# Moving low parts and a norm to GpSimd, issuing q's copies first and merging the shift transfers in a cross-attention and mixture-of-experts kernel

## The reference

```python
x = x + xattn(layernorm(x), ctx)      # then x = x + expert_ffn(layernorm(x))
# xattn:
q = ln_head((x @ Wq + bq)) ; k = ln_head(y_main @ Wk + bk) ; v = y_main @ Wv + bv   # 240 keys
k_dca, v_dca = ln_head(...), ...                                                      # 16 more keys
ctx     = softmax(q @ k.T * SCALE) @ v
ctx_dca = softmax(q @ k_dca.T * SCALE) @ v_dca
return (ctx + ctx_dca) @ Wo + bo
```

## Time and profile before

| what | value |
|---|---|
| median of three runs (lowest to highest) | 1104.68 us (1100.12 to 1105.48) |
| the profiled execution | 1106.82 us |
| its span, first to last instruction | 1105.0 us |
| granted TensorE clock, mean | 0.929 |
| TensorE busy | 948.3 us, 86% |
| VectorE busy | 797.6 us, 72% |
| ScalarE busy | 640.0 us, 58% |
| GpSimd busy | 285.1 us, 26% |

### The profile page before, as it was taken

One profiled execution on the slowest core, in us unless ns is written; L12 is line 12 of the kernel. 1 busy time (PEld: TensorE's weight loads), 2 busy tenths in 40 slices (PEclk: granted clock), 3 DMA queues, 4 the chain that ended last, 5 costly groups with the idle time before them and its releaser, 6 DMA issues. The chain is left out here.

```text
span 1105.0 us, 17666 instructions
## 1 busy us (share of the span) xinstructions
PE 948.3 (86%) x5148; PEld 674.2 (61%) x5148; DVE 797.6 (72%) x1723; ACT 640.0 (58%) x1659; POOL 285.1 (26%) x203
## 2 busy tenths in 40 slices
PE   0667899989989988989989989676379999999998
PEld 0334555556556555555555556333369999999997
DVE  3726777778777877777777777551878787878785
ACT  0222887787887887787787788672533232323231
POOL 0465135235235225135135135000000000000000
PEclk9977899999999999999999899777589999999999
DMA  7006435436435535445435435558211111111111
GB/s 266 28 20 144 103 91 158 118 92 159 120 95 153 130 92 146 112 99 158 114 99 157 105 88 131 138 180 261 84 39 58 57 57 57 57 57 57 57 38 39
DMA packets 56413, 116.41 MB, mean 105 GB/s; under 512 B 13944, under 2 KB 22392, under 8 KB 56120
## 3 DMA queue, kind: packets, MB, share of 16 engines
q1 hardware_dynamic: 53760, 115.16, 37.6%
q10 hardware_dynamic: 2616, 0.79, 0.3%
HBM read 47.24 MB, written 17.30 MB: 58 GB/s over the span
## 5 line engine op out<-in xcount | busy, mean ns | idle before, releaser
L477 POOL TENSOR_TENSOR vs<-vs,neg_half 128x16 f32<-128x16 f32 x66 | 191.0, 2916 | 391.9 <-DVE vs L934 391.9
L806 ACT ACTIVATE sc<-sc,nm 128x240 f32<-128x240 f32 x512 | 223.2, 444 | 46.2 <-DVE ed L982 45.4
L977 DVE TENSOR_REDUCE pm<-sc 128x64 f32<-128x1024 f32 x128 | 156.6, 1223 | 69.5 <-PE sc L633 65.2
L584 PE MATMUL ring<-wq,xT 128*128 128x512 f32 x256 | 142.5, 708 | 22.8 <-ACT xT L774 18.4
L633 PE MATMUL sc<-KS,QS 96*128 96x256 f32 x512 | 109.5, 339 | 54.8 <-ACT sc L806 44.1
L815 ACT ACTIVATE pt<-sc 128x1024 f32<-128x1024 f32 x128 | 124.2, 1024 | 33.7 <-PE sc L654 33.7
L1421 ACT ACTIVATE hb<-hb 128x352 f32<-128x352 f32 x64 | 31.9, 498 | 186.9 <-DVE hb L1477 186.9
L633 PEld LDWEIGHTS sc<-KS,QS 96*128 96x128 f32 x512 | 75.8, 201 | 98.8 <-ACT sc L806 60.1
L686 PE MATMUL ring<-wo,ot 128*128 128x512 f32 x256 | 124.7, 612 | 0.7 <-DVE ot L1030 0.7
L806 ACT ACTIVATION_READ_ACCUMULATOR sc<-sc,nm 128x1 f32 x512 | 110.8, 216 | 0.0
L584 PEld LDWEIGHTS ring<-wq,xT 128*128 128x128 f32 x256 | 55.8, 230 | 88.3 <-issue 63.8
(11 more groups left out here) (144 smaller groups left out, 1796.8 us busy)
## 6 DMA issues: line engine op xcount, KB each, us to landing
KS<-k_hi SPq DMA_DIRECT2D x128, 128.0 KB, 2.3
QS<-q_hi SPq DMA_DIRECT2D x128, 128.0 KB, 3.9
xin<-in_x_dram SPq DMA_DIRECT2D x16, 512.0 KB, 4.0
KS<-k_lo SPq DMA_DIRECT2D x64, 128.0 KB, 2.3
QS<-q_lo SPq DMA_DIRECT2D x64, 128.0 KB, 3.5
xres<-in_x_dram SPq DMA_DIRECT2D x16, 512.0 KB, 4.1
x_scratch<-xres SPq DMA_DIRECT2D x16, 512.0 KB, 4.3
x<-x_scratch SPq DMA_DIRECT2D x16, 512.0 KB, 3.2
```

What stands on the lines that cost most here:

```text
L477: pool.tensor_tensor(w, w, neg_half[0:rows, :], ALU.pow).then_inc(rstd, 1)
L584: last = pe.matmul(bank[:, :], xT[:, kc, t * P:(t + 1) * P], wq[:, kc, :], start=(kc == 0), stop=(kc == KC - 1))
L806: last = act.activation(s, s, ACT.Exp, bias=nm[:, t, h:h + 1], accum_out=den[:, t, h:h + 1])
L977: dve.tensor_reduce(pieces, s.rearrange("p h (c n) -> p h c n", n=DCA), AX_X, ALU.max, negate=True).then_inc(g_max, 1)
```

## The change

The low parts k_lo and q_lo and k's norm are computed by GpSimd and no longer by VectorE. VectorE makes q_hi right after score tile 1, where k's norm stood. SyncE issues q's copies ahead of k's, and in the order q_hi, q_lo, k_hi, k_lo; ctx is loaded before the residual's input. The two parts of the shift go in one transfer each, and not in two: s_hi into rows 96 and 97 of `QS`, s_lo into rows 98 and 99, where before s_hi had rows 96 and 98. The pattern in `KS` is changed to match, and is filled in 8 pieces for each of the two buffers and not in 4. One semaphore `split` becomes five.

```diff
-    def shift_rows(eng, par, a, part, row):
-
-        row += BLK + 2 * a
-        eng.dma_start(QS[par][row:row + 1, :, :, :].rearrange("p h g n -> p (h g) n").bitcast(F32),
-                      part[a * H:(a + 1) * H, :].bitcast(F32)).then_inc(sh_in, 16)
+    def shift_rows(eng, par, part, row):
+
+        eng.dma_start(QS[par][BLK + row:BLK + row + 2, :, :, :].rearrange("p h g n -> p (h g) n").bitcast(F32),
+                      part[:, :].bitcast(F32)).then_inc(sh_in, 16)
...
                 for n, (rows, first, end, value) in enumerate((
-                        (4, 0, KEYS, 0.0), (2, 0, KEYS, 1.0), (4, KEYS, TOK, 1.0), (2, KEYS, TOK, 0.0))):
-                    wait(pool, ones, 4 * i + n)
+                        (4, 0, KEYS, 0.0), (3, 0, KEYS, 1.0), (2, 0, KEYS, 0.0), (1, 0, KEYS, 1.0),
+                        (4, KEYS, TOK, 1.0), (3, KEYS, TOK, 0.0), (2, KEYS, TOK, 1.0), (1, KEYS, TOK, 0.0))):
+                    wait(pool, ones, 8 * i + n)
...
+        def q_low(m):
+
+            pool.wait_ge(q_hi_rdy, m + 1)
+            pool.tensor_tensor(q_lo[:, :, :], qf[:, :, :], q_hi[:, :, :].bitcast(F32),
+                               ALU.subtract).then_inc(q_lo_rdy, 1)
...
+        def normalise_k(m):
+
+            pool.wait_ge(rstd, norms(m) + T + NC)
+            for c in range(NC):
+                w, values = vs[0:ROWS[c], T + c, :], head_norm_values(T + c)
+                pool.tensor_tensor(values, values, w.unsqueeze(2).broadcast_to(values.shape),
+                                   ALU.mult).then_inc(k_norm, 1)
...
             if step in KEYED:
                 dca_keys(b + 1)
+                q_low(b + 1)
+                k_low(b + 1)
...
                 for k in range(T, T + NC):
                     root(k, norms(b + 2) + k, ROWS[k - T])
+                normalise_k(b + 2)
...
             if attn:
                 wait_evac(act, step, "LT", b)
-                for a in range(2):
-                    shift_rows(act, par, a, s_lo, 1)
+                shift_rows(act, par, s_lo, 2)
...
             if attn:
                 group_max(b, 1)
             if keyed:
-                for k in range(T, T + NC):
-                    normalise(k, norms(b + 1) + k, head_norm_values(k))
+                q_high(b + 1)
...
             if keyed:
-                split_k_high(step, b)
+                k_high(step, b)
...
-            if keyed:
-                split_k_low(b)
-            if attn:
                 dca_sums(b, 1)
-            if keyed:
-                split_q(b + 1)
```

More of the change, by code:

```diff
@@ L328, in norms, with q_norms @@
         return ND + 4 * m if not isinstance(m, int) or m > 0 else 0
+    def q_norms(m):
+        return ND + T * m if not isinstance(m, int) or m > 0 else 0
     def by_head(columns):
@@ L419, in body @@
             if step in KEYED:
-                sp.wait_ge(split, 4 * (b + 1) + 1)
+                sp.wait_ge(q_hi_rdy, b + 2)
+                stack_rows(QS, 1 - par, q_hi, 0, q_in)
+                stack_rows(QS, 1 - par, q_hi, 2, q_in)
+                sp.wait_ge(q_lo_rdy, b + 2)
+                stack_rows(QS, 1 - par, q_lo, 1, q_in)
+                sp.wait_ge(k_hi_rdy, b + 2)
                 stack_rows(KS, 1 - par, k_hi, 0, k_in)
                 stack_rows(KS, 1 - par, k_hi, 1, k_in)
-                sp.wait_ge(split, 4 * (b + 1) + 2)
+                sp.wait_ge(k_lo_rdy, b + 2)
                 stack_rows(KS, 1 - par, k_lo, 2, k_in)
@@ L426, in body @@
                 sp.wait_ge(sh_hi, b + 1)
-                for a in range(2):
-                    shift_rows(sp, par, a, s_hi, 0)
+                shift_rows(sp, par, s_hi, 0)
             if step in STATS:
                 load_x(b + 4)
-            if step in KEYED:
-                sp.wait_ge(split, 4 * (b + 1) + 3)
-                stack_rows(QS, 1 - par, q_hi, 0, q_in)
             if step in WOUT:
@@ L436, in body @@
                 sp.dma_start(x2_dram[b - 1], xres[:, :, :]).then_inc(x2_st, 16)
[L437 to L440, removed]
+            if step in PROJ and step != "late":
+                wait_full(sp, step, "CT", b)
+                sp.dma_start(cin[:, :, :], ctx_t[b + 3]).then_inc(c_ld, 16)
             if step in WOUT:
@@ L508, in body @@
                 selectors()
-                pool.wait_ge(ones, 8)
+                pool.wait_ge(ones, 16)
                 for j in range(2):
@@ L614, in k_transposes @@
         def k_transposes(step, b):
-            pe.wait_ge(norm, ND + 4 * (b + 2))
+            pe.wait_ge(k_norm, NC * (b + 2))
             for j in range(2):
@@ L1001, in bias_k, with q_high, k_high @@
                               kv_half(bkv_b[0:ROWS[c], :], 0), ALU.add).then_inc(taken(step, f"K{c}"), 1)
[L1003 to L1018, removed]
+        def q_high(m):
+            wait(dve, q_in, STACKED * m)
+            dve.tensor_copy(q_hi[:, :, :], qf[:, :, :]).then_inc(q_hi_rdy, 1)
+        def k_high(step, b):
             for name in ("KT0", "KT1"):
@@ L1022, in split_k_high @@
             dve.wait_ge(kd_rdy, b + 2)
-            split_high(b + 1, kf, k_hi, k_in)
-        def split_k_low(b):
-            split_low(b + 1, 0, kf, k_hi, k_lo)
+            wait(dve, k_in, STACKED * (b + 1))
+            dve.tensor_copy(k_hi[:, :, :], kf[:, :, :]).then_inc(k_hi_rdy, 1)
         def ctx_out(step, b, g):
```

23 lines of the change are left out of this document (12 added, 11 removed).

## The result

The changed kernel takes 1116.97 us (median of 4 runs, 1114.79 to 1118.94) where the kernel before takes 1104.63 (4 runs, 1100.12 to 1105.48): a ratio of 1.0118, 95% interval 1.0077 to 1.0159, so 12.3 us slower. The forecast was +6.2 us, 1110.9, range 1102 to 1118. The profiled runs lie closer together, 1106.82 and 1114.79: before's was above its median and after's was the lowest of its four.

What follows compares the result with a forecast made beforehand. TensorE fills 37.99 of an attention step's 41.28 us and waits 9.9 us in all for q_lo's copies. Fills +11.7, q's copies -9.9 and shift +4.4 gave +6.2 us on 1104.7: 1110.9 us, range 1102 to 1118.

Steps and rivals of the forecast that it cites:

- q's copies first: Attention steps: issuing q's copies ahead of k's removes TensorE's whole wait for q_lo, -9.9 us.
- The moved VectorE work and GpSimd's, nothing: Attention steps: 3.7 us a step off VectorE gains nothing, and GpSimd's 7.2 us more stays hidden; price 0.
- part 3: GpSimd in the attention steps: its 7.2 us of new work is hidden; the trace shows no slowdown of VectorE beside roots.
- The fills, +11.7: Start: eight more selector fills add 14.8 us, less 3.1 us of work no longer on the path, +11.7 us.
- The shift, +4.4: Attention steps: two-row transfers lie on two queues and land 0.44 us later, +4.4 us over sixteen steps.
- Of this the 13 steps that don't wait pay 0.44 - 0.2 = 0.24, so 3.1 us: Shift in steady steps: 0.44 us of lateness less 0.2 us to spare becomes time in 13 steps, 3.1 us.
- The clock rival: Attention steps: the changed pace keeps TensorE's clock up in 12 steps, 6.2 - 12 = -5.8 us, 1098.9; chance 0.06.
- the selectors-only rival: Another wait takes the place of q's, so its gain is lost: +11.7 + 4.4, 1120.8 us; chance 0.06.

Runs made afterwards that it cites:

- e5: The changed kernel run again, unchanged, on another chip: 1113.90 us against 1106.65 for the kernel before, ratio 1.0066.
- e3: The kernel before with each of its eight selector fills made twice, nothing else: 1118.85 us, ratio 1.0137 to the kernel before.
- e2: The changed kernel with all sixteen fills and its new row order, but four shift transfers of one row each: 1106.14 us, ratio 1.0022 to the kernel before.
- e1: The changed kernel with the old shift: four one-row transfers, old row order, eight fills: 1091.46 us, ratio 0.9884 to the kernel before.
- e4: e1 with k's norm and k_lo back on VectorE, only q_lo staying on GpSimd: 1092.43 us, ratio 0.9897 to the kernel before.
- e9: e2 with s_lo's issue held until an added 128x384 ScalarE copy is done: ratio 1.0039 to the kernel before.
- e12: e9 with a 128x768 copy instead of 128x384 ahead of s_lo's issue: ratio 1.0200 to the kernel before.
- e6: e2 with an added 128x640 ScalarE copy ahead of s_lo's issue, without a wait for it: ratio 0.9998 to the kernel before.
- e8: e1 with its eight fills moved to earlier places behind GpSimd's row roots: 1087.35 us, ratio 0.9809 to the kernel before.
- e7: The changed kernel with its sixteen fills moved to earlier places behind GpSimd's row roots: 1104.45 us, ratio 0.9975 to the kernel before.
- e10: The changed kernel with the 512 KB load of the next x issued behind the context's load: ratio 1.0121 to the kernel before.
- e11: The kernel before with only the two-row shift transfers, new row order and sixteen fills: ratio 1.0154 to the kernel before.

## Why the prediction was right in direction and short in size

The direction was right, and so were the mechanisms of the start and of q's copies. That the sum came within 1.5 us of the difference of the profiled runs (7.7) is partly luck. The start cost 10.8 us where 11.7 was said, and the steps gave back 3.1 us where 9.9 - 4.4 = 5.5 was said. The medians differ by 12.3 us in one set of runs and by 7.3 in the other (e5).

**q's copies first.** Said -9.9 us; e3 against e2, which differ by this and the move to GpSimd with the same sixteen fills and single rows, give 573.7 - 563.8 = -9.9 us in the fourteen steps, and 4.4 us more ahead of them. The wait for q_lo is gone and no other wait took its place: the mechanism is right. That the number is met to a tenth is luck. The q waits of e3 are 7.9 us and not 9.9, and the rest of the difference is pace; against the trace of the kernel before, the fourteen steps of e1 are shorter by 10.8 us and those of e2 by 12.9.

**The moved VectorE work and GpSimd's, nothing.** e4 confirms it in time, for k's norm and k_lo. But the reason that part 3 gave, that the trace shows no hindrance, was read from the wrong pair. The normalising of q beside GpSimd's roots was not slowed; the casts to a high part beside GpSimd's 128x1024 operations are, 0.69 to 1.5 us in a step and to 2.71 at the start. There the rule of the Trainium skill ("SBUF — State Buffer", the port pair is an exclusive lock) agrees with the trace: the cast ends after GpSimd's operation does (100.64 after 100.09, and 491.06 after 490.51 in the step shown). That the steps don't pay is the slack in front of the fourth tile; the start pays 2.0 us.

**The fills, +11.7.** Their price is right (14.8 said, 14.9 and 14.7 by e3 and e1/e2). The first scores moved by 10.4 us: fills 15.3 us longer, their start 2.35 us earlier in this run, which the prediction took as fixed (e5's second batch is 1.9 us later than after's), 3.1 us less for what left the path as said, and 2.0 us more for the slowed cast, which no step of the working had; 1.4 us came back between the q projection and the scores, for no reason that was looked for.

**The shift, +4.4.** As a sum of waits it measured 4.8 us in the fourteen steps, by terms that were off and cancelled. The slack is about 0.9 us and not 0.2: the 2.44 us from the issue's end to the scores, taken from a step in which TensorE had stood idle for 4.55 us, are not what a steady step needs (1.71 to 1.72 us in e9, 1.61 in e12's row at 649.13). Against e2 the closing writes end 0.6 to 0.9 us later, and not 0.44, since half of the pieces take 61 to 120 ns and not 48. And the scores start 1.0 to 1.6 us behind them where 0.8 us or less is enough for one-row transfers (e9, e12), a term that the working did not have.

The step of the working that failed most is the one from waits to time: "Of this the 13 steps that don't wait pay 0.44 - 0.2 = 0.24, so 3.1 us". It took the rest of the step as fixed. In the new order without the two-row transfer a step takes 40.67 us, and two or three of thirteen run at 2.4 GHz throughout, 39.2 to 39.5 us (e1, e2, e4, e6, e8, e9); with it none does, in three kernels and four traces (after, e5, e7, e10). That is 4.9 us in the sum of the steps, and the whole of the transfer costs 7 to 11 us by the medians.

The clock rival had the right mechanism, steps that gain or lose the full clock, but asked only whether the new order might gain some. The new order with one-row transfers has 2 or 3 of thirteen at a granted clock of 1.00, the old order 1 or 2 (before, e3, e11), so such a gain is not shown; what is shown is that the two-row transfer takes them away in the new order. In the old order it does not (e11, two).

What decides this stays open. It is not the mean length of the steps alone: with 40.9 to 41.0 us no step runs at full clock in after, e5, e7 and e10, with 41.0 to 41.1 us two do in e3 and e11, and with 41.7 us six do in e12. Nor is it a wait for the shift as such (e10 has next to none, e12 has long ones). Another wait did take up what the shift cost in the old order (e11), which is what the selectors-only rival said of q's gain; in the new order none did.

## What to carry to other kernels

A transfer merged from several rows saves an issue of 0.6 us and may lose its spread over the queues; count the packets of the queue before and after, and look where its last closing write ends. Set-up work goes where its engine is idle (here 5 us and 58 us), before asking what it should cost: e7 won 9.5 us with it. A small transfer that is issued just behind a large load can land behind it (e12), so a delay may cost nothing up to a point and much more than itself beyond it. A wait added in a step that waits elsewhere too can change nothing (e11). Where the granted clock varies from step to step, a few tenths of a us can cost more than themselves; price such an edit in the surroundings it will have, and count the steps at full clock as well as the waits.

## What the runs showed of the hardware

A transfer to 2 rows x 16 pieces of 1 KB runs on two queues: its closing writes end 2.1 to 2.3 us behind the issue's end, and the reader starts 3.1 to 3.9 us behind it. With two transfers of one row these are 0.92 us, and 1.7 us in e9 where the reader was just held up (2.3 to 2.4 us where TensorE had been idle for 4.4 us). Transfers of 16 KB whose pieces would have begun just behind the first of a 512 KB load began 1.3 to 1.6 us later (e12).

A GpSimd fill of 1 to 4 rows costs its width alone: 3.29 us for 3840 columns and 0.31 us for 256, a start every 1.85 us on the mean. One fill of 3 rows took 3.73 us, with a cast of VectorE beside its start. A ScalarE copy does not hold up a transfer that ScalarE issues behind it (e6); a wait for it does.

VectorE's cast of 128x1024 from 4-byte SBUF data takes 0.69 us alone. When GpSimd had started first it ended 0.55 us after GpSimd's operation, whatever was left of that: 3.26 us at 67.99 (a fill until 70.69), 2.71 us at 97.93 and 1.53 us at 489.53. A VectorE multiplication of 128x512 with two SBUF inputs took 0.68 to 0.72 us beside GpSimd's roots, in 20 cases of the kernel after.
